# A Swin block on one core: the MLP of chunks 0 to 2 laid beside the last chunk's end, in three pairs of PSUM banks

## The reference

```python
xw = windows of x                      # (256 windows, 64 tokens, 32 channels)
h = _ln(xw, ln1_g, ln1_b)
q, k, v = split(h @ qkv_w.T + qkv_b)   # 4 heads of 8
attn = softmax(q * hd ** (-0.5) @ k^T + bias[rpb])
o = (attn @ v) @ proj_w.T + proj_b
xw = xw + o
h = _ln(xw, ln2_g, ln2_b)
h = gelu(h @ fc1_w.T + fc1_b)          # 32 -> 128, the exact gelu
h = h @ fc2_w.T + fc2_b                # 128 -> 32
out = xw + h, back to (4, 32, 64, 64)
```

## Time and profile before

| what | value |
|---|---|
| median of 3 runs | 177.25 us (176.6 to 177.63) |
| profiled execution | 178.3 us |
| its span | 176.6 us |
| TensorE matmul busy | 156.7 us (89%) |
| ScalarE busy | 128.2 us (73%) |
| VectorE busy | 118.9 us (67%) |
| GpSimd busy | 91.1 us (52%) |

### The profile page before, as it was taken

How to read it: one execution, slowest core, us unless ns; L and a number is a source line. 1 busy time by engine, 2 the same in 40 slices (tenths; PEclk the granted TensorE clock), 3 DMA queues, 4 the chain that set the end, 5 groups by cost and what they waited for, 6 DMA issues and landing times.

```text
span 176.6 us, 6351 instructions
## 1 busy us (share of the span) xinstructions
PE 156.7 (89%) x2688; PEld 86.7 (49%) x2688; DVE 118.9 (67%) x220; ACT 128.2 (73%) x180; POOL 91.1 (52%) x103
## 2 busy tenths in 40 slices
PE   7978699999999999999999999999999794749972
PEld 7535354764575556457555754664575350111210
DVE  4556996969777896979597787969788702303332
ACT  4344967759697798769687977878683459788991
POOL 7500658638584947657585848668587420020000
PEclk9999999999999999999999999999999999988999
DMA  2760000000000000000000000000000000101333
GB/s 75 222 206 0 4 2 4 4 0 4 6 4 0 4 0 4 6 2 4 4 4 0 4 4 2 4 4 4 2 4 4 0 4 0 59 0 59 123 119 119
DMA packets 3245, 4.71 MB, mean 27 GB/s; under 512 B 946, under 2 KB 1298, under 8 KB 3218
## 3 DMA queue, kind: packets, MB, share of 16 engines
q1 hardware_dynamic: 2840, 4.23, 7.1%
q0 software_dynamic: 256, 0.07, 0.3%
q10 hardware_dynamic: 122, 0.01, 0.1%
HBM read 2.21 MB, written 2.10 MB: 24 GB/s over the span
## 4 chain that ended last, share of the span: by engine, by line
PE 57%; ACT 26%; DVE 7%; issue 7%; ACTq 1%; POOLq 1%; DVEq 0%
PE ps L694 14%; ACT pt L260 11%; PE ps L604 9%; PE ps L712 7%; PE ps L678 7%; PE ps L719 5%; ACT hid L350 4%; DVE s_sb L485 4%; ACT v_blk L313 3%; PE ps L757 3%; PE ps L771 3%; PE ps L653 3%; PE ps L586 2%; ACT rstd L339 2%; PE ps L610 2%
## 5 line engine op out<-in xcount | busy, mean ns | idle before, releaser
L215 POOL TENSOR_TENSOR s_sb<-s_sb,mx 128x512 f32<-128x512 f32 x64 | 66.1, 1042 | 46.9 <-DVE mx L495 46.9
L485 DVE TENSOR_TENSOR s_sb<-ps,bias_t 128x512 f32<-128x512 f32 x64 | 43.7, 683 | 12.4 <-PE ps L678 12.4
L495 DVE TENSOR_REDUCE mx<-s_sb 128x8 f32<-128x512 f32 x64 | 43.9, 686 | 2.2
L260 ACT ACTIVATE pt<-ps 128x1024 f32<-128x1024 f32 x32 | 32.7, 1021 | 12.9 <-PE ps L694 12.7
L694 PEld LDWEIGHTS ps<-ident,s_sb 128*128 128x128 f32 x256 | 27.4, 140 | 22.5 <-issue 20.7
L694 PE MATMUL ps<-ident,s_sb 128*128 128x128 f32 x256 | 35.2, 279 | 2.1 <-ACT pt L260 1.4
L678 PE MATMUL ps<-k_m,q_sb 32*64 32x256 f32 x512 | 18.5, 386 | 2.4 <-DVE att L515 1.4
L712 PEld LDWEIGHTS ps<-pt,v_blk 128*32 128x32 f32 x1024 | 15.2, 110 | 9.7 <-ACT pt L260 9.2
L712 PE MATMUL ps<-pt,v_blk 128*32 128x64 f32 x1024 | 17.8, 221 | 1.3 <-ACT pt L260 0.3
L610 PE MATMUL ps<-x_sb,cent_m 64*64 64x512 f32 x64 | 18.0, 640 | 0.9 <-DVE x_sb L521 0.9
L350 ACT ACTIVATE hid<-ps,fb 128x512 f32<-128x512 f32 (+1 forms) x16 | 16.8, 1110 | 1.8 <-PE ps L757 1.8
(11 more groups left out here) (92 smaller groups left out, 180.2 us busy)
## 6 DMA issues: line engine op xcount, KB each, us to landing
x_sb<-in_x_dram SPq DMA_DIRECT2D x8, 256.0 KB, 4.9
out_dram<-y_sb SPq DMA_DIRECT2D x7, 256.0 KB, 2.0
out_dram<-y_sb SPq DMA_DIRECT2D x2, 128.0 KB, 1.8
raw_b<-in_L_conv_rpb_dram POOLq DMA_DIRECT2D x8, 8.0 KB, 2.8
f_nat<-in_L_conv_fc_w_dram SPq DMA_DIRECT2D x2, 16.0 KB
w_nat<-in_L_conv_qkv_w_dram ACTq DMA_DIRECT2D x1, 12.0 KB
p_nat<-in_L_conv_proj_w_dram SPq DMA_DIRECT2D x1, 4.0 KB
vec_r<-in_L_conv_ln_g_dram ACTq DMA_DIRECT2D x1, 0.1 KB
```

The costliest lines, as they stand in the source:

```text
L215: pool.tensor_tensor(tile, tile, mx[:, n % 4, :].unsqueeze(2).to_broadcast([128, 2 * NH, NT]), ALU.subtract).then_inc(shifted, 1)
L260: act.activation(pt[:, n % 8:n % 8 + 2, :, :, :].rearrange("p u a k n -> p (u a k n)"), ps[:, 4:6, :].rearrange("p u n -> p (u n)"), ACT.E ...
L485: dve.tensor_tensor(s_sb[:, n % NSB, :, :, :].rearrange("p a h m -> p a (h m)"), S_PS[g].rearrange("p (a k) -> p a k", a=2), bias_t[:, :, ...
L495: dve.reduce_max(mx[:, n % 4, :], s_sb[:, n % NSB, :, :, :].rearrange("p a h m -> p (a h) m"), AX.X)\
```

## The change

In the loop's step c = 8, where chunk 7 (p = NCH - 1) comes to its end, TensorE now does up(1) ahead of project, up(2) ahead of center2, and down(0) and down(1) at the step's end, both into bank 4. ScalarE does gelu of chunks 0, 1 and 2 in one row behind the last exp. Their ups write pairs of banks: 0 to 3 for chunk 0, 2, 3, 5, 6 for chunk 1, and 0, 1, 5, 6 for chunk 2; each gelu is two instructions over two banks each. hid has three buffers. The tail behind the loop begins with up(3) and keeps its banks.

The reciprocal of chunk 7's second sums is one VectorE instruction (inv_den_last), and so is its square (square2_last). inv_std2(6) moves ahead of the last exp. The table of Ln and Exp is loaded at the beginning of step c = 9. down(1) waits for add_y(0), up(4) for add_y(2), since these share bank 4.

```diff
-        hid = sb("hid", [128, 2, G, TC])
+        hid = sb("hid", [128, 3, G, TC])
...
+        def hidden_banks(c):
+            return {0: (0, 1, 2, 3), 1: (2, 3, 5, 6), 2: (0, 1, 5, 6)}.get(c, (0, 1, 2, 3) if c % 2 else (3, 4, 5, 6))
+
+        def gelu_parts(c):
+            early = {0: ((2, 4), (0, 2)), 1: ((2, 4), (0, 2)), 2: ((0, 2), (2, 4))}
+            return early.get(c, ((3, 4), (0, 3)) if c % 2 else ((0, 1), (1, 4)))
+
+        def y_bank(c):
+            return 4 if c < 3 else 7
...
-                if c >= 2:
-                    act.wait_ge(down_ready, c - 1)
...
+                if c >= 3:
+                    act.wait_ge(down_ready, c - 2)
+                for first, last in gelu_parts(c):
+                    bank = hidden_banks(c)[first]
+                    act.activation(hid[:, c % 3, first:last, :].rearrange("p g n -> p (g n)"),
+                                   ps[:, bank:bank + last - first, :].rearrange("p g n -> p (g n)"),
                                    ACT.Gelu, bias=fb1[:, :]).then_inc(gelu_ready, 1)
...
+                if p == NCH:
+                    act.preload_act_table_set("natural_log_exp_and_others")
                 if there(p - 1):
                     log_var2(p - 1)
+                if p >= NCH - 1:
+                    inv_std2(p - 1)
                 if there(p):
                     exp_round(p, 3)
...
-                if there(p - 1):
+                if there(p - 1) and p < NCH - 1:
                     inv_std2(p - 1)
-                if there(p):
+                if there(p) and p < NCH - 1:
                     inv_den(p, 1)
                 if p == NCH - 1:
                     act.preload_act_table_set("gelu_and_others")
                     gelu(0)
-                    act.preload_act_table_set("natural_log_exp_and_others")
+                    gelu(1)
+                    gelu(2)
...
-                if there(p):
+                if there(p) and p < NCH - 1:
                     square2(p)
...
             act.preload_act_table_set("gelu_and_others")
-            for c in range(1, NCH):
+            for c in range(3, NCH):
                 gelu(c)
...
+            def inv_den_last():
+                dve.wait_ge(summed, 2 * NCH)
+                dve.reciprocal(den[:, 1, :], OD_PS[1][:, 256:512]).then_inc(den_ready, 1)
+
+            def square2_last():
+                dve.wait_ge(kept2, NCH)
+                dve.tensor_tensor(sq2[:, :], h2_sb[:, NCH - 1, :], h2_sb[:, NCH - 1, :], ALU.mult).then_inc(squared2, 1)
...
+                if p == NCH - 1:
+                    inv_den_last()
                 if there(p):
                     divide(p, 1)
...
                 if there(p):
                     keep2(p)
+                if p == NCH - 1:
+                    square2_last()
...
-                elif c == 1:
-                    pe.wait_ge(gelu_ready, 2)
                 else:
                     pe.wait_ge(gelu_ready, 2 * c - 1)
...
+                if c == 4:
+                    pe.wait_ge(y_ready, 3)
...
-                elif bank == 7:
+                elif bank == y_bank(c):
                     pe.wait_ge(y_ready, c)
...
+                if p == NCH - 1:
+                    up(1)
...
+                if p == NCH - 1:
+                    up(2)
...
                 if p == NCH - 1:
-                    down(0, 4, slice(0, TC))
+                    down(0, y_bank(0), slice(0, TC))
+                    down(1, y_bank(1), slice(0, TC))
...
-            up(1)
-            for c in range(1, NCH - 1):
+            for c in range(2, NCH - 1):
                 up(c + 1)
-                down(c, 7, slice(0, TC))
+                down(c, y_bank(c), slice(0, TC))
```

More of the change, by code:

```diff
@@ L564, in _ @@
             for c in range(NCH - 1):
-                add_y(c, 7 if c else 4, c, slice(0, TC))
+                add_y(c, y_bank(c), c, slice(0, TC))
             add_y(NCH - 1, 7, NCH - 1, slice(0, TC // 2))
@@ L747, in up @@
                     pe.wait_ge(divided, 2 * NCH - 1)
-                elif c == 1:
-                    pe.wait_ge(gelu_ready, 2)
                 else:
                     pe.wait_ge(gelu_ready, 2 * c - 1)
-                if c == 2:
-                    pe.wait_ge(y_ready, 1)
+                if c == 1:
+                    pe.wait_ge(expd, NU)
                     pe.wait_ge(k_copied, NCH)
                     pe.wait_ge(k_scaled, NCH - 1)
+                if c == 4:
+                    pe.wait_ge(y_ready, 3)
                 for g in range(G):
-                    ins = pe.matmul(ps[:, first_bank(c) + g, :], f1_s[C * g:C * (g + 1), :],
+                    ins = pe.matmul(ps[:, hidden_banks(c)[g], :], f1_s[C * g:C * (g + 1), :],
                                     h2_sb[C * g:C * (g + 1), c, :], start=True, stop=True, tile_position=(C * g, 0))
@@ L764, in down @@
                     pe.wait_ge(expd, NU)
-                elif c == 1:
+                elif c == 3:
                     pe.wait_ge(log2, NCH)
-                elif bank == 7:
+                elif bank == y_bank(c):
                     pe.wait_ge(y_ready, c)
@@ L770, in down @@
                     to = C * (g ^ 2)
-                    ins = pe.matmul(ps[to:to + C, bank, cols], f2_st[:, :], hid[:, c % 2, g, cols],
+                    ins = pe.matmul(ps[to:to + C, bank, cols], f2_st[:, :], hid[:, c % 3, g, cols],
                                     start=True, stop=True, tile_position=(0, to))
```

## The result

| | before | changed |
|---|---|---|
| median, first comparison (4 runs each) | 177.22 us | 174.78 us |
| median, second comparison (17 and 6 runs) | 177.51 us | 174.70 us |
| profiled execution, span | 178.3, 176.6 us | 174.56, 172.8 us |

The ratio is 0.9877 (95% interval 0.9833 to 0.9921) in the first comparison and 0.9848 (0.9809 to 0.9886) in the second: 2.2 to 2.7 us faster. The prediction was 174.6.

The account below looks back on a forecast made before the run. ScalarE bounds the even tail at 2.19 us a chunk. Two chunks fewer (4.38) plus the slow start (1.28), less 3.03 for a longer stage in front, give 2.63: 177.25 to 174.6 us, 8-in-10 range 173.0 to 176.1.

Parts of the forecast that it names:

- The reciprocal: Chunk 7's last sums on VectorE: eight passes, 2.26 us, up to 0.95 hidden and the other 1.3 on the path.
- Rival 1: At chunk 7's last sums: the reciprocal is one pass, 0.42 us, all behind 1.05 us earlier, median 173.6; chance 26%.
- The new wait of down(1): At step c = 8's end: down(1) waits for add_y(0) in bank 4, delaying variance2(7); 1.7 us on the path.
- The gelus in pairs: ScalarE's gelus as two pieces of two banks cost what one and three banks cost, 2.12 us a chunk.
- the square: Chunk 7's square on VectorE: 0.68 us against 0.64 on ScalarE, at least 0.63, at most 0.75.
- The sum: At the start of gelu(3): 159.11 instead of 161.74 us, 2.63 earlier, with the 14.86 us behind it unchanged.
- the order and the clock: Up to gelu(3): the gain's two parts, 1.35 us from the order of work, 1.28 from the tail's slow start.
- Rival 2: In the tail, at up(4): TensorE's clock falls all the same and 1.28 us are lost again, median 175.9; chance 13%.
- Rival 3: From project on: clock falls to 1.2 GHz, five groups cost 3.7 to 4.0 us, median 179.7, slower than before; chance 5%.
- Rival 4: Whole kernel: no gain that counts, bank 4's wait growing to 4 us or the reciprocal to 4.9, 177.2; chance 6%.

Follow-up runs that it names:

- e7: Changed kernel with a copy in place of chunk 7's reciprocal, the division of its second half left out; 174.21 us, 0.9837 of before.
- e3: Changed kernel with down(1) behind variance2(7) instead of ahead of it; 172.76 us, 0.9757 of before.
- e8: Changed kernel with a second reciprocal of the same elements on VectorE ahead of the one that counts; 178.30 us, 1.0067 of before.
- e1: Changed kernel with the reciprocal of the last sums as Ln and Exp on ScalarE again; 178.26 us, 1.0059 of before.
- e9: Kernel before with matmuls of zeros: 4 behind attend(7, 1), 2 ahead of center2, 8 behind up(1); 176.84 us, 1.0008 of before.
- e10: e1 with 12 matmuls of zeros on TensorE ahead of up(1) in step c = 8; 177.41 us, 1.0019 of the kernel before.
- e4: Kernel before with 8 matmuls of zeros behind up(1); 176.50 us, 0.9971 of before.

## Why the prediction was right

Its times, moved by the 0.75 us of the common part, against the changed kernel's:

| step | forecast | measured |
|---|---|---|
| last large exp | 142.36 | 142.37 |
| reciprocal | 145.46, 2.26 long | 145.46, 1.76 long |
| project | 148.22 | 147.80 |
| center2 | 150.30 | 149.87 |
| square done | 152.83 | 152.41 |
| down(1) | 153.59 | 153.22 |
| variance2(7) | 154.58 | 154.22 |
| gelu(3) | 158.36 | 158.00 |
| gelu(3) to the end | 14.86 | 14.80 |

*The reciprocal* is the one term that was off, by 0.50 us: 1.76 for 256 columns. By the line of one pass (0.16 us plus 1.02 ns a column) it is 6.1 passes, neither one nor eight. An estimate by the repeat count of 8 in the Trainium skill ("VectorE: DVE Perf Modes", section "First, the fixed hardware budget") is 2.3 us, so the measurement is under it. Everything behind moved by 0.36 to 0.43 us and kept its distances. Rival 1 is out (1.76, not 0.42), and its price was a little high: it put 1.05 us between 2.26 and 0.42, where 0.36 (2.26 to 1.76) and 0.44 (e7) make 0.80 at gelu(3).

*The new wait of down(1)* was priced at 1.7 us on the path; e3 took it away and gelu(3) came 1.74 earlier. *The gelus in pairs* cost 2.12 as said, *the square* 0.69.

*The sum* was 2.63 and the stretch from variance2(6) to gelu(3) gave 2.99, 0.36 of it from the reciprocal. The medians moved by 2.4 to 2.8, so the median's forecast came out nearer than the term allows: the executions around the profiled ones vary by more than that. That it came within 0.2 us of 174.78 and 174.70 is in part luck. The forecast took one lost stretch of clock in the run before and none in the changed kernel, which is what most runs did, but not all, and the order and the clock, its two parts, are not 1.35 and 1.28 in the timed runs (below).

*Rival 2, the clock in the tail*, given 13%, is what two of ten runs show in their mean clock and their 176.7 us, where the rival said 175.9; none of these was profiled, so the place of the fall is not shown. *Rival 3* didn't come in the changed kernel, but e8 and e1 show its fall at project, though for three groups (e8) and two (e1) and not for the five that it priced: the forecast stood nearer to that edge than its 5% say. With 2.4 us of idle ahead of project instead of 0.8 the kernel is slower than before (e8). *Rival 4* is out: both intervals lie below 1. One reading was wrong without weight: the first steps of the loop that the change leaves alone are eight (c = 0 to 7), not seven.

What the prediction did not see in this form is how the gain splits. It put the clock at 1.28 and the order at 1.35 (2.63 - 1.28). In the profiles it is 1.29 (e9 against before) and 1.70 (19.71 - 18.01); in the timed runs at full clock on both sides the order is worth 1.0 us. Against e1 the order alone is 2.6 in the traces and 2.3 in the runs that kept their clock (e10). The first two, 1.70 and 1.0, don't agree, and with starts and last stores that vary by over half a microsecond the runs don't settle it further.

## What to carry to other kernels

Two edits that each look like a gain can both lose alone: here early MLP work needs the table switch free of the sums, and the longer reciprocal that frees it needs the MLP work to cover TensorE's idle time. When work is pulled forward into a wait, look at what it is queued ahead of: one matmul group that waited for a shared bank, standing ahead of the step that all others waited for, took 1.7 us back. And fill a stretch of waiting with work that TensorE has to do anyway before trying matmuls of zeros, which kept the clock in the profiles of e9 and e10 but moved the medians of the three kernels that had them by only 0.4 to 0.85 us.

## What the runs showed of the hardware that was not expected

- RECIPROCAL of 128x256 fp32 from PSUM on VectorE takes 1.76 us, 4.2 times the 0.42 of a copy or a product of that size.
- The same program loses TensorE's clock in one execution and not in the next: the kernel before kept it in 4 of 63 runs, the changed one in 8 of 10. And it falls at different places: at up(2) (156.9 us) in the kernel before's profile; at center2 (148.05) in e4's, whose program is the same up to there.
- Two executions of programs that are the same up to 140 us differ there by up to 1.5 us: 1.2 of it is there at the first square, and from it to variance2(6) they still differ by 0.4 us (132.99 to 133.41).
